# A routed expert layer on one core: one early code visit, one word of sizes, rotations ahead of the ranks, a last tile added by block

## The reference

```python
x_right = hamilton(x_filtered, q_right_conj)
x_rotated = hamilton(q_left_n, x_right)
...
logits = jnp.einsum('bsd,de->bse', x, router_w) + router_b
top1 = jnp.argmax(softmax(logits), axis=-1)
for i in range(8):
    h = jnp.einsum('bsd,df->bsf', x, w1[i]) + b1[i]      # 256 -> 2048
    a, g = jnp.split(h, 2, axis=-1)
    y = jnp.einsum('bsh,hd->bsd', a * sigmoid(g), w2[i]) + b2[i]
    out = out + jnp.where((top1 == i)[..., None], y, 0.0)
return x + out                                           # x here is the unrotated input
```

## Time and profile before

| what | value |
|---|---|
| median of 3 runs | 208.42 us (208.19 to 209.0) |
| the profiled execution | 207.35 us |
| its span, first to last instruction | 205.6 us |
| busy: PE, PE weight loads, DVE, ACT, POOL | 93%, 88%, 71%, 61%, 43% |
| mean granted clock of TensorE | 0.994 of full speed |
| DMA traffic | 42.34 MB, mean 206 GB/s |

### The profile page before, as it was taken

The page is one execution under the profiler, slowest core; times in us unless marked ns, Lnnn a source line. Parts: engine busy times, 40 slices in busy tenths (PEclk is TensorE's granted clock), DMA queues, the critical chain, the costliest instruction groups (busy, mean ns, idle before and its releaser), DMA issues.

```text
span 205.6 us, 4304 instructions
## 1 busy us (share of the span) xinstructions
PE 191.6 (93%) x1451; PEld 181.2 (88%) x1453; DVE 146.1 (71%) x296; ACT 125.1 (61%) x222; POOL 87.7 (43%) x138
## 2 busy tenths in 40 slices
PE   7997867999999999999999999999999999999960
PEld 3777733999999999999999999999999999999950
DVE  4928944678854888398869869995999488839510
ACT  2454770385756676486875958695777667648310
POOL 8002544631700645445467084555637364004403
PEclk9999999999999999999999999999999999999997
DMA  4999925879948161787198469618861976001001
GB/s 136 383 402 385 311 64 190 261 260 328 308 128 357 51 213 47 249 333 238 34 390 302 154 199 406 232 38 303 344 205 53 336 277 208 0 0 37 28 5 43
DMA packets 20054, 42.34 MB, mean 206 GB/s; under 512 B 2472, under 2 KB 14905, under 8 KB 17978
## 3 DMA queue, kind: packets, MB, share of 16 engines
q1 hardware_dynamic: 15808, 31.54, 42.8%
q0 software_dynamic: 4000, 10.50, 16.1%
q10 hardware_dynamic: 218, 0.01, 0.1%
HBM read 35.74 MB, written 8.13 MB: 213 GB/s over the span
## 4 chain that ended last, share of the span: by engine, by line
PE 90%; DMA 4%; issue 1%; DVE 1%; POOL 1%; ACT 1%; DVEq 0%; POOLq 0%
PE y_ps L1208 8%; PE g_ps L1176 8%; PE g_ps L1169 8%; PE a_ps L1169 8%; PE y_ps L1210 8%; PE a_ps L1176 8%; PE y_ps L1209 8%; PE a_ps L1172 8%; PE g_ps L1172 8%; PE y_ps L1120 3%; PE y_ps L942 3%; DMA x_turn<-x_rows,g_idx 2%; PE a_ps L1018 2%; PE a_ps L1099 2%; DMA x_rows<-arena 2%
## 5 line engine op out<-in xcount | busy, mean ns | idle before, releaser
L854 DVE SCALAR_TENSOR_TENSOR arena<-a_ps,b_t,arena 128x336 f32<-128x336 f32 (+1 forms) x64 | 33.3, 521 | 27.7 <-PE a_ps L1176 24.1
L579 ACT ACTIVATE arena<-g_ps,b_t 128x336 f32<-128x336 f32 (+1 forms) x64 | 32.2, 503 | 32.4 <-PE g_ps L1176 32.2
L452 POOL DMA_INDIRECT out_dram<-x_turn,s_idx x22 | 28.5, 1295 | 47.3 <-DVE x_turn L874 35.4
L740 DVE TENSOR_TENSOR w_lo<-w_raw,w_hi 128x1024 fp32r<-128x1024 f32 x32 | 37.7, 1221 | 9.1 <-DMA x_turn<-x_rows,g_idx 5.2
L438 POOL DMA_INDIRECT x_turn<-x_rows,g_idx x24 | 30.6, 1275 | 31.1 <-DMA out_dram<-x_turn,s_idx 17.3
L1208 PE MATMUL y_ps<-u_hi,w_hi 128*128 128x336 f32 (+2 forms) x128 | 38.1, 298 | 0.3 <-issue 0.3
L1210 PE MATMUL y_ps<-u_lo,w_hi 128*128 128x336 f32 (+2 forms) x128 | 37.5, 293 | 0.0
L1209 PE MATMUL y_ps<-u_hi,w_lo 128*128 128x336 f32 (+2 forms) x128 | 37.5, 293 | 0.0
L1169 PE MATMUL g_ps<-xr_hi,w_hi 128*128 128x336 f32 (+2 forms) x128 | 36.1, 299 | 0.0
L1169 PE MATMUL a_ps<-xr_hi,w_hi 128*128 128x336 f32 (+2 forms) x128 | 35.6, 294 | 0.0
L1172 PE MATMUL a_ps<-xr_hi,w_lo 128*128 128x336 f32 (+2 forms) x128 | 35.5, 293 | 0.0
(11 more groups left out here) (181 smaller groups left out, 306.8 us busy)
## 6 DMA issues: line engine op xcount, KB each, us to landing
w_raw<-in_L_ffn_w_dram SPq DMA_DIRECT2D x16, 1024.0 KB, 7.9
w_raw<-in_L_ffn_w_dram SPq DMA_DIRECT2D x16, 512.0 KB, 4.6
x_own<-in_x_dram SPq DMA_DIRECT2D x4, 512.0 KB, 6.0
x_rows<-x_own SPq DMA_DIRECT2D x4, 512.0 KB, 11.1
x_rows<-arena SPq DMA_DIRECT2D x8, 256.0 KB, 3.4
x_turn<-x_rows,g_idx POOLq DMA_INDIRECT x24, 6.0
out_dram<-x_turn,s_idx POOLq DMA_INDIRECT x22, 3.7
x_own<-x_rows,g_idx POOLq DMA_INDIRECT x8, 5.6
```

The lines of the kernel that those rows point to most:

```text
L579: nc.scalar.activation(sig[:, c % SIG_RING, 0:n], pair[c % RING][1][:, 0:n], ACT.Sigmoid, bias=b1_t[:, bass.ds(e * (2 * NC) + (NC + c), 1) ...
L740: V.tensor_tensor(unit_of(w1_lo, u), raw_unit(u), unit_of(w1_hi[:, :].bitcast(F32), u), ALU.subtract)\
L854: V.scalar_tensor_tensor(u32[:, c % (8 - SIG_RING), 0:n], pair[c % RING][0][:, 0:n], b1_t[:, bass.ds(e * (2 * NC) + c, 1)], sig[:, c % SIG ...
```

## The change

- **One visit.** Five visits go. The one that stays, at the start, lands behind leaf 1 (272 columns), just ahead of the code of leaf 2 (336). The five warm-ups ahead of the spread go, and so do the two long ones behind the last visit.
- **One word.** DVE packs all eight sizes into one word, `packed`, ahead of the one-hots of the spare slots; each field is 4 minus the size's number, 0 stands for "special". PE waits for `packed_ready` and loads it once. The number of the last tile is read only in "special". The start waits for `y_done` besides.
- **Order on PE.** The `wr` product stands behind f = 6. Pairs 1, 2 and 3 are rotated ahead of the rank matmul.
- **Last tile.** ACT biases 224 instead of 336 columns, the second half in two pieces (128, then the rest). PE turns the first half into `y_ps` at once, and each block of the second half into a PSUM bank of its own (`apart`). DVE adds the first half of all blocks in one operation and the second by block.

The diff, cut to its core:

```diff
+        apart = turn_ps[0:NSUB]
...
-                nc.gpsimd.memset(places[:, e:e + 1], float(1 << (LEFT * (e - 1))) if e > 0 else 0.0)
+                nc.gpsimd.memset(places[:, e:e + 1], -float(PLACES[e]))
...
                 if i >= NE - 1:
-                    for h in range(KH):
-                        biased(i, e, h, 0, FIRST, yt_done[h])
+                    biased(i, e, 0, 0, min(n, FIRST), yt_done[0])
+                    biased(i, e, 1, 0, P, yt_first)
+                    biased(i, e, 1, P, min(n, FIRST), yt_done[1])
...
             indices(early_ps[:, 0:FX], 0, FX)
-            subtile_one_hot(q_oh_spare, FX, TS - FX, q_spare).then_inc(q_oh_spare_ready, 1)
-
-            dve.wait_ge(spare_ready, 1)
...
+            link(V.tensor_tensor(places[:, :], places[:, :], steps, ALU.mult))
+            link(V.tensor_reduce(left, places[:, :], AX.X, ALU.add))
+            V.tensor_scalar(packed[:, :], left, float(len(SIZES) * sum(PLACES)), None, ALU.add).then_inc(packed_ready, 1)
+            subtile_one_hot(q_oh_spare, FX, TS - FX, q_spare).then_inc(q_oh_spare_ready, 1)
+
+            dve.wait_ge(spare_ready, 1)
...
+            def add_by_block(i, blocks, done):
 
                 for s in range(blocks):
                     dve.wait_ge(gathered[s], (i + 1) * 16)
-                dve.wait_ge(y_turned, i + 1)
+                rows = rows_of(i)
+                dve.wait_ge(half_turned, i - NE + 2)
+                V.tensor_tensor(rows[:, 0:blocks, 0], y_half[0][:, 0:blocks * P].rearrange("p (s d) -> p s d", d=P),
+                                rows[:, 0:blocks, 0], ALU.add)
                 for s in range(blocks):
-                    rows, y = rows_of(i, s, 1)
-                    V.tensor_tensor(rows[:, 0], y[:, 0], rows[:, 0], ALU.add).then_inc(last_added, 1)
+                    dve.wait_ge(block_turned, (i - NE + 1) * NSUB + s + 1)
+                    last = V.tensor_tensor(rows[:, s, 1], apart[s][:, 0:P], rows[:, s, 1], ALU.add)
...
             visit(1)
             pe.wait_ge(still_set, 1)
-            keep_warm(early_ps, 5)
...
-                if f == 3:
-                    visit(2)
-                if f == 4:
+                if f == 6:
                     pe.wait_ge(wr_loaded, 16)
...
-            rotate_blocks(1)
+            for b in range(1, GROUPS):
+                rotate_blocks(b)
             pe.wait_ge(consts_ready, CONSTS)
             pe.wait_ge(in_row_ready, 1)
...
-            pe.wait_ge(ctrl_ready, 1)
-            last_tile = load_last(pe)
-            visit(6)
-            keep_warm_long(late_ps, 2)
-            LANDING_AT = {(0, 7): 3, (1, 2): 4, (2, 3): 6}
...
+            pe.wait_ge(packed_ready, 1)
...
-            pe.reg_load(word_reg, ctrl[0:1, 1:2])
-            pe.reg_mov(size_reg, f_size(reg(word_reg, 127)))
-            pe.reg_load(left_reg, ctrl[0:1, 2 + TAB:3 + TAB])
+            pe.reg_load(left_reg, packed[0:1, 0:1])
+            pe.reg_mov(size_reg, reg(left_reg, 1 << 30) & ((1 << LEFT) - 1))
+            pe.reg_mov(left_reg, reg(left_reg, 1 << 30) >> LEFT)
...
                     pe.br("top")
+                    if low == 1:
+                        landing_behind(1)
...
-            turn_back_rows(NSUB)
+            pe.wait_ge(yt_done[0], at1)
+            for s in range(NSUB):
+                last = T.transpose(y_half[0][:, s * P:(s + 1) * P], yt[:, s * P:(s + 1) * P], ident[:, :])
+            last.then_inc(half_turned, 1)
+            for s in range(NSUB):
+                if s < 2:
+                    pe.wait_ge((yt_first, yt_done[1])[s], at1)
+                T.transpose(apart[s][:, 0:P], yt[:, ITEM + s * P:ITEM + (s + 1) * P], ident[:, :]).then_inc(block_turned, 1)
+            pe.wait_ge(ctrl_ready, 1)
+            last_tile = load_last(pe)
...
+            pe.wait_ge(y_done, at1)
             for s in range(TURNED - 1):
                 turn((s,), first16, end=False)
                 keep_warm_long(late_ps, 1)
```

More of the change, by code:

```diff
@@ L55, in adaln_moe_ffn_kernel @@
     LEFT = 3
-    SPECIAL = len(SIZES)
+    PLACES = [1 << (LEFT * e) for e in range(NE)]
     EPS = 1e-8
@@ L1233, in leaf, with jump, by_size @@
                 second_half(size, 1)
-            def by_size(size, low, high):
-                if low == high:
-                    if low == SPECIAL - 1:
-                        with pe.If(size >= SPECIAL):
-                            here = nc.cur_bb
-                            pe.br("special")
-                            nc.switch_bb("behind_special", parent=here)
+            def jump(to, behind):
+                here = nc.cur_bb
+                pe.br(to)
+                nc.switch_bb(behind, parent=here)
+            def by_size(code, low, high):
+                if low == high:
                     leaf(low)
```

83 lines of the change are left out of this document (35 added, 48 removed).

## The result

The changed kernel takes **215.11 us** (median of 4 runs, 212.92 to 215.69); the kernel before, run beside it, 208.71 us. The ratio is 1.028, with a 95% interval of 1.019 to 1.037: slower by 1.9 to 3.7%. The forecast was 206.8, with a range of 206.0 to 208.6, so it was wrong in sign and by 8.3 us. The profiled execution took 215.03 us, with a span of 213.2 (before 205.6).

What follows compares the result with a forecast made beforehand. TensorE's matmuls were taken as the bound (90% of the path), so only front and tail could move: gather -0.5 and tail -1.1 give -1.6 us, from the 208.42 median to 206.8; range 206.0 to 208.6.

Steps and rivals of the forecast that it cites:

- The visit: At the start of PE's program: one jump to code not yet fetched, starting at 0.9 us, would take 3.4 us.
- the way back: PE's return jump from the early visit, at the start: forecast at 0.2 us.
- the spread: PE's spread of the quaternions, in the front: would start at 4.8 us instead of 3.82, 1.0 later.
- The early visit, and what goes with it: Front of PE: one far visit kept, five visits and five warm-ups dropped; logits turned back at 16.7 us, 1.0 later.
- the gather's 0.5 us: Gather of the first tile's rows would start 0.5 us earlier, and everything to the last matmul would shift with it.
- rival (b): At the start, the visit's way back misses too, a second 3.4 us: 210.2 us, slower than before; chance 0.07.
- The rotations: Pairs 2 and 3 ahead of the ranks: last row write at 27.1 instead of 27.58, gather 0.5 us earlier.
- The front: PE's work before the gather, from the spread to the logits' turning back: 1.0 us later because of the visit.
- The word: One packed word of sizes, built by VectorE and loaded by PE: its cost hidden under other waits, nothing lost.
- The tail: Behind the last matmul: first scatter at 199.0 instead of 200.08, 1.1 us earlier, with the landings following.
- Rival (c): TensorE's clock falls before the first tile, in a longer lull with fewer warm-ups: 207.8 us, at most 209.1; chance 0.18.
- What would show it: Closing list of trace signs, such as first product 0.5 us earlier and a 3.4 us visit jump, and of contrary signs.

Runs made afterwards that it cites:

- e13: Changed kernel with its one far visit right ahead of the load of the word and "special" moved behind the leaves: 207.64 us, ratio 0.993.
- e10: Changed kernel with the early visit replaced by three later visits, each one block of code further than the last: 206.26 us, ratio 0.989.
- e5: Kernel before with only the new order: pairs 2 and 3 ahead of the rank matmul, `wr` product behind the seventh transposes: 208.33 us, ratio 1.000.
- e11: Kernel before with the new tail and without the five warm-ups ahead of the spread: 206.33 us, ratio 0.989.
- e15: Changed kernel, early visit kept, with the code of "special" moved behind the leaves: 211.23 us, ratio 1.012.
- e6: Kernel before with its six visits replaced by the one early visit, nothing else changed: 215.70 us, ratio 1.033.
- e4: Kernel before with only the new treatment of the last tile (the new tail): 206.20 us, ratio 0.989.
- e1: Changed kernel with the six old visits put back for the early one, warm-ups still dropped: 206.31 us, ratio 0.990.
- e7: Changed kernel with its one visit moved from the start to behind the index matmuls of the fixed slots, at 25.5 us: 213.20 us, ratio 1.025.
- e12: Changed kernel with its one far visit moved from the start to right ahead of the load of the word: 218.45 us, ratio 1.046.
- e8: Changed kernel with the six visits and all seven warm-ups of the kernel before put back: 207.33 us, ratio 0.993.
- e3: Changed kernel with the seven dropped warm-ups put back, its one early visit kept: 217.98 us, ratio 1.042.

## Why the prediction was wrong

**The visit: the step that failed.** Its price (3.4 us; measured 3.30), the way back (0.2; 0.19) and the spread (4.8; 4.60) were right. What failed is that the part "The early visit, and what goes with it" priced only the jump. It took for granted that a visit, once paid, has brought the code that the first tile needs, and set the five dropped visits at nothing. Neither was costed, and so the gather's 0.5 us could be passed on to the last matmul, "since PE waits for nothing between": it does wait between, for code. The rows for the doubt were there: 3,408 ns for the one place that nobody had visited, and 175 to 381 ns for all the others. The runs put in its place: the early visit instead of the six costs 215.11 - 206.31 = 8.8 us (8.0 by the ratios), by a hole of 3.3 behind the jump of 4.0, a stall of 1.0 and 3.4 of lower clock in the first tile. Another 1.0, between the traces of the two, is the third block's rows, turned at 36.83 instead of 35.86; no run ties that to the visit.

**The rule of the Trainium skill.** The Trainium skill ("Runtime: NRT & Kernel Launch", section "Instruction fetch mechanics") calls the prefetch purely sequential. The runs agree: three steps of neighbouring blocks cost 0.4 to 1.2 us each and leave the leaf in place, one jump over blocks costs 3.3 and, but for e13, leaves a hole in the first or the second tile. Its sentence of a store of two blocks was set aside because the jumps between tiles do not stall. That is right for the kernel before, and in e10 the code queue brings nothing from 53.7 to 199.7 us, over seven tiles. But what would follow from that sentence, that a far block is not kept, was the case here; rival (b) had it only for the way back.

**The rotations: -0.5, measured 0.0** (ratio 0.998 to 1.003, e5). The hole ahead of the ranks did close: in the changed kernel the rank matmul ran at 19.94 without idle time, as forecast:

```profile
19.94 0.17 PE L1039 MATMUL g_ps<-in_row,lower 128*128 128x8 bf16 x1
```

The step that failed here is that the last row write was taken to move with the last copy (27.58 - 0.5). In e5 the copy came 1.6 us earlier and the rows 0.3, because the queue of row writes took 4.31 us from there where it had taken 3.30; the gather took 0.9 longer besides. The prediction named the queue as the bound, at a gain of 1.1; it allowed less.

**The front: +1.0, no such effect found.** An earlier spread (e11) changes nothing. A later one, at 5.26 in e15, still has the rows written at 27.24 and the third block turned at 34.80, both ahead of before (27.58 and 35.23); at 6.77, in e6, they are written at 29.99. What goes with the rows over the traces is x: in the ten in which its last part landed before 10.8 us they are written at 26.8 to 27.7, in the six in which it landed after 11.2 at 27.9 to 29.2, e6 apart. That is an order of events, not a test. In the changed kernel's trace x landed at 12.19 (before 10.09), the logits were turned at 17.42 against a forecast 16.7, and the rows were written at 28.33 against 27.1.

**The word: 0;** nothing clear of noise speaks against it, and no run has it alone. **The tail: -1.1, measured -2.25.** The mechanism was right to 0.1 us (first scatter at 1.47 behind the last matmul, 1.5 forecast). The term left out the scatter's landing, which by the traces the fetch behind the jump to "done" had delayed; the prediction looked at that jump only as a cover for PE's load.

**Rival (c), the clock.** It did fall ahead of the first tile, at 26.1, but not for the reason given: it fell at 25.9 in e5, with all warm-ups in place, and at 27.3 in e4, whose front is that of before, for 3.4 us. The profiled execution of before, with a full clock there, was a favourable one: the mean clock of 23 other executions of that kernel was 0.977 to 0.994 against its 0.994. The fall that cost time was the second, at 39.8, behind the hole, and rival (c) did not have it.

**What would show it.** The last sentence of that part named the case: a first product that is not earlier, matmuls of the first tile at twice their time, a second long jump. All three came, and no rival joined them: rival (b) ended at 210.2, because it counted neither the second hole nor the clock behind it.

**A version that beats both.** e10, e1, e4 and e11 all take 206.2 to 206.3, some 1.1% below before; what they have in common is the new tail, and code brought in steps.

## What to carry to other kernels

A visit that warms code pays only if the code is still there when it is run: check the jump that uses it, not the jump that fetches it, and visit in steps of neighbouring blocks, which worked in every kernel here that did it. A hole in TensorE's work is to be priced with the lower clock behind it; here 4.3 us of holes cost 3.4 more. Before a term is summed against one profiled execution, see whether that execution is typical of the kernel's others.

## What the runs showed of the hardware

- A block of code that a far jump brought was gone 5.6 us after the way back in e7; in e12 it was there 3.6 us after the way back, and the second tile, some 24 us later, missed. Blocks brought one after another stayed for the whole of the loop (e1, e10).
- Code fetches come in pieces of 16 KB (nine, 0.15 MB in the changed kernel's page). The last small scatter landed 2.3 us behind its issue with none on the way, 2.5 to 2.7 with one under way at its issue, and 3.5 and 4.2 with one that began behind it; seventeen traces, no run made for it.
- TensorE's clock fell to the lower level near 26 us whether or not seven warm-ups were there (e4, e5, e8 with them, e1 without), though not in the profiled execution of before, and warm-up matmuls that run at that level take long enough to become the path themselves (e3: eight in 6.64 us, ahead of the first turn).
